# Moving small roundings, a subtraction and score copies from VectorE to ScalarE in a vision-transformer layer

## The reference

```python
h = relu(x @ W0.T) * (x @ W1.T) @ Wo.T          # token stage
h = concatenate([cls_tok, h])                   # 513 rows
h = h + attention(layernorm(h))                 # 16 heads of 16; every linear is quantised:
#   x_norm = (x - mean) * rsqrt(var + eps)      # mean, var over all rows of one image
#   y = round(x_norm * 127 / max|x_norm|) * max|x_norm| / 127  per row, times a ternary weight
h = h + moe(layernorm(h))                       # 8 experts, the best 2 of each row, silu(gate) * up
```

## Time and profile before

| | |
|---|---|
| median of 3 runs | 2325.64 us (2325.11 to 2326.09) |
| the profiled execution | 2323.41 us, span 2321.4 us |
| TensorE matmuls busy | 2018.8 us, 87% |
| TensorE weight loads busy | 1154.5 us, 50% |
| VectorE busy | 1572.5 us, 68% |
| ScalarE busy | 1235.4 us, 53% |
| GpSimd busy | 924.3 us, 40% |
| mean granted TensorE clock | 0.95 |

### The profile page before, as it was taken

The page is one execution under the profiler, slowest core; times in us unless marked ns, Lnnn a source line. Parts: engine busy times, 40 slices in busy tenths (PEclk is TensorE's granted clock), DMA queues, the critical chain, the costliest instruction groups (busy, mean ns, idle before and its releaser), DMA issues. The chain is left out here.

```text
span 2321.4 us, 49821 instructions
## 1 busy us (share of the span) xinstructions
PE 2018.8 (87%) x13328; PEld 1154.5 (50%) x13329; DVE 1572.5 (68%) x4268; ACT 1235.4 (53%) x2600; POOL 924.3 (40%) x958
## 2 busy tenths in 40 slices
PE   4789999898998998999989998884139999999997
PEld 2343443344443444444444443232128988888885
DVE  4477888887887888788787889973264444444443
ACT  0246666565665556656566566663145554545553
POOL 2222233433333234232342334333146666666653
PEclk9899999999999999999999999997569999999999
DMA  2312322223232223222232322310243333333331
GB/s 88 101 56 69 97 74 80 83 73 82 74 88 75 77 76 88 75 83 75 70 89 73 86 75 79 79 34 28 100 159 65 64 63 63 62 63 62 63 59 22
DMA packets 171886, 172.31 MB, mean 74 GB/s; under 512 B 30786, under 2 KB 160404, under 8 KB 171668
## 3 DMA queue, kind: packets, MB, share of 16 engines
q1 hardware_dynamic: 141396, 134.87, 20.1%
q0 software_dynamic: 30272, 34.80, 9.3%
HBM read 100.70 MB, written 68.99 MB: 73 GB/s over the span
## 5 line engine op out<-in xcount | busy, mean ns | idle before, releaser
L1162 DVE TENSOR_REDUCE mxs<-bank 128x1 f32<-128x512 f32 x1024 | 696.6, 684 | 218.1 <-PE bank L503 198.8
L833 ACT ACTIVATE pt<-bank 128x512 f32<-128x512 f32 x1024 | 588.5, 594 | 371.4 <-PE bank L512 368.2
L503 PE MATMUL bank<-ks,qs 96*128 96x512 bf16 x1024 | 400.2, 392 | 80.0 <-DVE mxs L1162 60.3
L512 PE MATMUL bank<-qs,ks 99*128 99x512 bf16 x1024 | 395.2, 387 | 9.8 <-ACT pt L833 9.2
L1780 PE MATMUL bank<-xh,gu_h 128*128 128x256 bf16 (+1 forms) x1152 | 309.6, 269 | 3.6 <-issue 1.9
L1780 PE MATMUL bank<-xl,gu_h 128*128 128x256 bf16 (+1 forms) x1152 | 308.4, 268 | 0.0
L1780 PE MATMUL bank<-xh,gu_l 128*128 128x256 bf16 (+1 forms) x1152 | 308.2, 268 | 0.0
L1740 POOL DMA_INDIRECT out<-y_sb,ids x136 | 217.2, 1597 | 203.2 <-ACT y_sb L1831 178.7
L521 PE MATMUL bank<-pt,v_sb 128*32 128x512 f32 x2048 | 279.5, 619 | 0.0
L503 PEld LDWEIGHTS bank<-ks,qs 96*128 96x128 bf16 x1024 | 103.7, 101 | 349.7 <-DVE mxs L1162 234.0
L1888 DVE TENSOR_TENSOR hid_e<-bank,act_g 128x256 f32<-128x256 f32 (+1 forms) x288 | 116.9, 406 | 170.0 <-PE bank L1780 166.5
(11 more groups left out here) (290 smaller groups left out, 3443.5 us busy)
## 6 DMA issues: line engine op xcount, KB each, us to landing
qs<-qk_dram SPq DMA_DIRECT2D x128, 128.0 KB, 2.6
ks<-qk_dram SPq DMA_DIRECT2D x64, 192.0 KB, 3.3
xt<-x_t SPq DMA_DIRECT2D x16, 512.0 KB, 3.9
h_dram<-h_sb SPq DMA_DIRECT2D x16, 512.0 KB, 3.5
qs<-qk_dram SPq DMA_DIRECT2D x128, 64.0 KB, 2.3
ks<-qk_dram SPq DMA_DIRECT2D x64, 128.0 KB, 3.3
hw<-h_dram SPq DMA_DIRECT2D x16, 512.0 KB, 4.2
out<-hw SPq DMA_DIRECT2D x16, 512.0 KB, 3.0
```

Of the source, the lines that this page charges most:

```text
L503: mm(score[u % 2][:, :], qs[0:QK, h, blk(t)], ks[0:QK, h, :], start=True, stop=True) \
L512: mm(scoret[u % 2][:, :], ks[0:QK + MROWS, h, blk(t)], qs[0:QK + MROWS, h, :], start=True, stop=True).then_inc(s("pe_st"), 1)
L833: f(pt[:, t % 2, j, :], scoret[u % 2][:, :], ACT.Exp).then_inc(s("act_exp"), 1)
L1162: v.reduce_max(mxs[:, t, g * GH + j:g * GH + j + 1], score[u % 2][:, :], AX.X).then_inc(s("dve_mx"), 1)
```

## The change

Four pieces of VectorE's work go to ScalarE; the numbers computed are the same.

- The negation of the maxima with its rounding (was L1172) is done by ScalarE at u = 0 of the next group, the second rounding (was L1179) at u = 2. VectorE forms `dsc` and `nmr` at u = 1 and the third part at u = 3.
- The three `scs` copies at slot 13 are done by ScalarE; `mc` stays on VectorE, at slot 14, after them.
- The subtraction of the mean from `oc` is done by ScalarE at slot 53, as an addition of `nms2` by its bias; the reduction moves to slot 54.
- The semaphores follow: VectorE's two chain semaphores of the maxima go, `dve_mf`, `act_nh`, `dve_nr`, `act_nm`, `act_scs`, `act_ocm` come.

```diff
@@ ScalarE
+                    if u == 0 and mt[0].ok:
+                        b, gg = mt
+                        wait(act, s("dve_mf"), NG, b, gg + 1)
+                        wait(act, s("pe_mt"), NG, b, gg)
+                        f(nmp[:, :, 0:GH], mf[:, :, heads(gg)], ACT.Copy, scale=-1.0).then_inc(s("act_nh"), 1)
+                    if u == 2 and mt[0].ok:
+                        b, gg = mt
+                        wait(act, s("dve_nr"), NG, b, gg + 1)
+                        f(nmp[:, :, GH:2 * GH], nmr[:, :, :], ACT.Copy).then_inc(s("act_nm"), 1)
...
+                    if C.ok and at == 13:
+                        wait(act, s("pe_t7"), 1, C, 1)
+                        wait(act, s("dve_dsc"), NG, C, -NG)
+                        for k in range(2):
+                            f(scs[:, C.par, k * TB * NH:(k + 1) * TB * NH].rearrange("p (a t h) -> p a t h", a=2, h=NH),
+                              d2[:, 0:S // 2].rearrange("p (t k a h) -> p k a t h", t=2, k=2, a=2)[:, k, :, :, 0:NH],
+                              ACT.Copy).then_inc(s("act_scs"), 1)
+                        f(scs[:, C.par, 2 * TB * NH:(2 * TB + 1) * NH], d2[:, S // 2:S // 2 + NH], ACT.Copy).then_inc(s("act_scs"), 1)
...
+                    if W.ok and at == 53:
+                        cflat = oc[:, :, :].rearrange("p j d -> p (j d)")
+                        wait(act, s("dve_nms2"), 1, W, 1)
+                        f(cflat, cflat, ACT.Identity, bias=nms2[0:NG, :]).then_inc(s("act_ocm"), 1)
@@ VectorE
-        def negate_maxima(b, g):
+        def largest(b, g):
             wait(dve, s("dve_mx"), UNITS * NG, b, UNITS * (g + 1))
-            ch = Link("dve_chain_m", NG * 4, b, 4 * g)
+            if g == 0:
+                wait(dve, s("act_scs"), 3, b, 3)
...
-            ch(v.tensor_tensor(mf[:, :, hs], mxs[:, :, hs], scl, ALU.max))
-            wait(dve, s("pe_mt"), NG, b, g)
-            ch.go(v.tensor_scalar(nmp[:, :, 0:GH], mf[:, :, hs], -1.0, None, ALU.mult))
+            v.tensor_tensor(mf[:, :, hs], mxs[:, :, hs], scl, ALU.max).then_inc(s("dve_mf"), 1)
         def maxima_rest(b, g):
-            ch = Link("dve_chain_m", NG * 4, b, 4 * g + 2)
-            ch.hold()
-            ch(v.scalar_tensor_tensor(nmr[:, :, :], mf[:, :, heads(g)], -1.0, nmp[:, :, 0:GH], ALU.mult, ALU.subtract))
-            ch.go(v.tensor_copy(nmp[:, :, GH:2 * GH], nmr[:, :, :]))
...
+            wait(dve, s("dve_mf"), NG, b, g + 1)
+            wait(dve, s("act_pcls"), NG, b, g + 1 - NG)
+            v.tensor_tensor(dsc[:, :, hs], scl, mf[:, :, hs], ALU.subtract).then_inc(s("dve_dsc"), 1)
+            wait(dve, s("act_nh"), NG, b, g + 1)
+            v.scalar_tensor_tensor(nmr[:, :, :], mf[:, :, hs], -1.0, nmp[:, :, 0:GH], ALU.mult, ALU.subtract) \
+                .then_inc(s("dve_nr"), 1)
         def maxima_low(b, g):
+            wait(dve, s("act_nm"), NG, b, g + 1)
             v.tensor_tensor(nmp[:, :, 2 * GH:3 * GH], nmr[:, :, :], nmp[:, :, GH:2 * GH], ALU.subtract).then_inc(s("dve_nm"), 1)
-            wait(dve, s("act_pcls"), NG, b, g + 1 - NG)
-            v.tensor_tensor(dsc[:, :, hs], scl, mf[:, :, hs], ALU.subtract).then_inc(s("dve_dsc"), 1)
...
-                    if u == 0 and mt[0].ok:
+                    if u == 1 and mt[0].ok:
                         maxima_rest(*mt)
-                    if u == 1 and mt[0].ok:
+                    if u == 3 and mt[0].ok:
                         maxima_low(*mt)
...
-                    if C.ok and at == 13:
-                        wait(dve, s("pe_t7"), 1, C, 1)
-                        for k in range(2):
-                            v.tensor_copy(scs[...], d2[...]).then_inc(s("dve_scs2"), 1)
+                    if C.ok and at == 14:
+                        wait(dve, s("act_scs"), 3, C, 3)
                         v.tensor_reduce(out=mc[:, :], in_=d2[:, CM_AT:CM_AT + 2 * VW].rearrange("p (a h) -> p h a", a=2)[:, 0:NH, :],
                                         axis=AX.X, op=ALU.max).then_inc(s("dve_mc"), 1)
-                        wait(dve, s("dve_scs2"), 2, C, 2)
-                        signal(v.tensor_copy(scs[:, C.par, 2 * TB * NH:(2 * TB + 1) * NH], d2[:, S // 2:S // 2 + NH]),
-                               "dve_scs", 1, C, 1)
...
-                    if W.ok and at == 53:
+                    if W.ok and at == 54:
                         cflat = oc[:, :, :].rearrange("p j d -> p (j d)")
-                        signal(v.tensor_scalar(cflat, cflat, ms2[0:NG, 0:1], None, ALU.subtract), "dve_ocm", 1, W, 1)
+                        wait(dve, s("act_ocm"), 1, W, 1)
                         wait(dve, s("pe_amc"), 1, W, 0)
```

More of the change, by code:

```diff
@@ L631, in body @@
                             if C.ok:
-                                wait(pe, s("dve_scs"), 1, C, 1)
+                                wait(pe, s("dve_mc"), 1, C, 1)
                             else:
@@ L1162, in head_max, with maxima_low @@
             v.reduce_max(mxs[:, t, g * GH + j:g * GH + j + 1], score[u % 2][:, :], AX.X).then_inc(s("dve_mx"), 1)
-        def negate_maxima(b, g):
+        def largest(b, g):
             wait(dve, s("dve_mx"), UNITS * NG, b, UNITS * (g + 1))
-            ch = Link("dve_chain_m", NG * 4, b, 4 * g)
+            if g == 0:
+                wait(dve, s("act_scs"), 3, b, 3)
             hs = heads(g)
             scl = scs[:, b.par, 0:TB * NH].rearrange("p (t h) -> p t h", t=TB)[:, :, hs]
-            ch(v.tensor_tensor(mf[:, :, hs], mxs[:, :, hs], scl, ALU.max))
-            wait(dve, s("pe_mt"), NG, b, g)
-            ch.go(v.tensor_scalar(nmp[:, :, 0:GH], mf[:, :, hs], -1.0, None, ALU.mult))
+            v.tensor_tensor(mf[:, :, hs], mxs[:, :, hs], scl, ALU.max).then_inc(s("dve_mf"), 1)
         def maxima_rest(b, g):
-            ch = Link("dve_chain_m", NG * 4, b, 4 * g + 2)
-            ch.hold()
-            ch(v.scalar_tensor_tensor(nmr[:, :, :], mf[:, :, heads(g)], -1.0, nmp[:, :, 0:GH], ALU.mult, ALU.subtract))
-            ch.go(v.tensor_copy(nmp[:, :, GH:2 * GH], nmr[:, :, :]))
-        def maxima_low(b, g):
             hs = heads(g)
-            ch = Link("dve_chain_m", NG * 4, b, 4 * g + 4)
-            ch.hold()
-            v.tensor_tensor(nmp[:, :, 2 * GH:3 * GH], nmr[:, :, :], nmp[:, :, GH:2 * GH], ALU.subtract).then_inc(s("dve_nm"), 1)
             scl = scs[:, b.par, 0:TB * NH].rearrange("p (t h) -> p t h", t=TB)[:, :, hs]
+            wait(dve, s("dve_mf"), NG, b, g + 1)
             wait(dve, s("act_pcls"), NG, b, g + 1 - NG)
             v.tensor_tensor(dsc[:, :, hs], scl, mf[:, :, hs], ALU.subtract).then_inc(s("dve_dsc"), 1)
+            wait(dve, s("act_nh"), NG, b, g + 1)
+            v.scalar_tensor_tensor(nmr[:, :, :], mf[:, :, hs], -1.0, nmp[:, :, 0:GH], ALU.mult, ALU.subtract) \
+                .then_inc(s("dve_nr"), 1)
+        def maxima_low(b, g):
+            wait(dve, s("act_nm"), NG, b, g + 1)
+            v.tensor_tensor(nmp[:, :, 2 * GH:3 * GH], nmr[:, :, :], nmp[:, :, GH:2 * GH], ALU.subtract).then_inc(s("dve_nm"), 1)
         def normalise(b, g):
@@ L1372, in body @@
                                                ALU.subtract, ALU.max).then_inc(s("dve_am"), 1)
-                    if C.ok and at == 13:
-                        wait(dve, s("pe_t7"), 1, C, 1)
-                        for k in range(2):
-                            v.tensor_copy(scs[:, C.par, k * TB * NH:(k + 1) * TB * NH].rearrange("p (a t h) -> p a t h", a=2, h=NH),
-                                          d2[:, 0:S // 2].rearrange("p (t k a h) -> p k a t h", t=2, k=2, a=2)[:, k, :, :, 0:NH]) \
-                                .then_inc(s("dve_scs2"), 1)
+                    if C.ok and at == 14:
+                        wait(dve, s("act_scs"), 3, C, 3)
                         v.tensor_reduce(out=mc[:, :], in_=d2[:, CM_AT:CM_AT + 2 * VW].rearrange("p (a h) -> p h a", a=2)[:, 0:NH, :],
                                         axis=AX.X, op=ALU.max).then_inc(s("dve_mc"), 1)
-                        wait(dve, s("dve_scs2"), 2, C, 2)
-                        signal(v.tensor_copy(scs[:, C.par, 2 * TB * NH:(2 * TB + 1) * NH], d2[:, S // 2:S // 2 + NH]),
-                               "dve_scs", 1, C, 1)
                     if P.ok and at in (16, 17):
@@ L1517, in body @@
                     if u == UNITS - 1 and C.ok:
-                        negate_maxima(C, g)
+                        largest(C, g)
         if stage == STEPS:
```

## The result

The changed kernel took 2306.44 us, the median of 6 runs (2300.94 to 2313.08), beside 2325.38 us for the kernel before on the same chip (6 runs, 2323.05 to 2330.11): a ratio of 0.9918 (0.9896 to 0.9940), 19 us. The forecast was 2315.4, a gain of 10.2 us; the time lies at the lower end of the stated range (2303 to 2325), where the third rival had put it (2304, chance 0.15).

What follows compares the result with a forecast made beforehand. TensorE was taken as the pace, with VectorE setting the end in a few places per image. Gains 3.6 + 4.7 + 1.5 + 2 = 11.8 us less 1.6 made 10.2, from 2325.64 to 2315.4 us; range 2303 to 2325.

Steps and rivals of the forecast that it cites:

- the two checks on ScalarE: Signs of error: VectorE waiting over 0.2 us for each ScalarE rounding, or vcls released by ScalarE's own queue instead of fk.
- L608's wait in image 3: Sign of the forecast: this weight load's wait for VectorE, 1.07 us before, would fall below 0.6.
- rival C: VectorE's stalls beside GpSimd vanish, and three images lose half-clock stretches with shorter TensorE waits: -21 us, 2304, chance 0.15.
- Slots 48 to 53: Second rounding gone ahead of TensorE's wait for slot 51's maximum: 0.28 us in 13 images, gain 3.6 us.
- Slots 63 to 3: Chain work cut where TensorE needs kbd and qbd: 0.59 us in half of 16 images, gain 4.7 us.
- Slots 53 to 58: VectorE level with TensorE sooner after the subtraction goes: 0.1 us per image, gain 1.5 us, bounds 0 and 22.
- item 3: Slot 53: the subtraction L1497, mean 1396 ns, leaves VectorE, removing 1.4 us of its time per image.
- Slot 13: Copies worth 0.4 us leave VectorE, but it waits for TensorE in slot 14, so gain 0.
- The charge for ScalarE: Twelve added ScalarE instructions per image, 0.22 us each, charged at 0.1 us per image, 1.6 us; bounds 0 and 42.
- Last two images: From 1400 to 1558 us, about a quarter of 8.4 us removed from VectorE lands: gain 2 us.
- A: TensorE reaches slot 53 earlier but then waits elsewhere, so a third of the sum arrives: -3.5 us, 2322, chance 0.20.
- B: Slots 0 to 6: ScalarE becomes late, the chain behind it slips 0.8 us per image: +7.3 us, 2333, chance 0.08.

Runs made afterwards that it cites:

- e1: Kernel before with only the two roundings of the maxima moved to ScalarE (L1178 and L1186 later): 2311.15 us against 2325.82, ratio 0.9936.
- e6: The whole change except the class query's subtraction, which stays on VectorE in slot 53: 2299.90 us against 2318.82 of the kernel before, ratio 0.9911.
- e7: The whole change except the class score copies, which stay on VectorE: 2300.58 us against 2318.82 of the kernel before, ratio 0.9916.
- e8: Changed kernel with each of the two roundings done a second time on ScalarE into an unread tile: 2300.54 us, ratio 0.9917 to the kernel before.
- e3: Kernel before with only the class score copies of slot 13 moved to ScalarE: 2314.92 us against 2325.82, ratio 0.9944.
- e9: Kernel before with one added VectorE memset of one column in slot 13: 2315.43 us against 2322.66, ratio 0.9968.
- e12: Kernel before with three added VectorE memsets of one column each in slot 13: 2320.40 us against 2328.93, ratio 0.9969.
- e2: Kernel before with only the class query's mean subtraction (slot 53) moved to ScalarE, its maximum to slot 54: 2315.50 us against 2325.82, ratio 0.9961.
- e4: Kernel before with both roundings kept on VectorE, the chain spread one instruction each over slots 0 to 3 of the group: 2315.96 us against 2325.82, ratio 0.9952.
- e5: Kernel before with its two class score copies of slot 13 in swapped order, no work removed: 2321.25 us against 2318.82, ratio 1.0011.
- e11: Changed kernel with row counter, output scale and router's weights moved to other VectorE slots: 2288.39 us, ratio 0.9851 to the kernel before.

## Why the prediction was half right

The direction and the bounding views were right, and so were the two checks on ScalarE: fk still releases vcls, and no wait for a rounding appears. L608's wait in image 3 came to 0.68 us, where below 0.6 was expected (1.07 before). The forecast itself was 9 us too slow, nearly half of the gain, and that the range held owes something to luck: it reached so far down because of rival C, and a part of the gain is granted clock and two pauses, which no term of the sum had. By its own steps:

**Slots 48 to 53** (-0.28 x 13 = -3.6). The size is exact inside the loop: -0.28 us in the even images of the changed kernel and of e1, e6, e7 and e8. Images 2 and 13, outside it, gave 0.09 us each, so 10 images in place of 13 had the full gain. What the step left out is the odd images, -0.64: 0.36 us more in five images (1.8 us), from a pause that e3 takes away too without touching this stretch, and behind it the half-clock stretches of images 3, 5 and 9, some 1.7 us each (5.0 us). e3 shows both without the roundings. The wait that I expected at 0.95 us was 0.58 for that reason.

**Slots 63 to 3** (half of the images at -0.59: -4.7). This is the term that failed most by size: slots 0 to 7 gave 9.0 us in the profiled execution, stretches at half clock included. That in image 10 VectorE again waits for TensorE at the maximum of slot 0, "and nothing is left", was the wrong end of the thought. In the even images of the kernel before stood a later wait that begins with VectorE's fk, over ScalarE's vcls and the exps behind it, in slot 6:

```profile
1033.12 0.39 PE L512 MATMUL bank<-qs,ks 99*128 99x512 bf16 x1 [0.69 <-ACT pt L833]
```

I had used the 4.1 us of these waits as the thing at risk from ScalarE, and not as something to gain. In the changed kernel they are 0.2 us in one place. Part of it comes back as a wait for GpSimd in slot 1, 1.13 us in every even image from 4 to 12, where it had been 0 in three of them and 1.0 in two. The net is -0.56 us in the even images. Of the odd ones image 3 shows -1.00 with no pause ahead of it, and image 13 -1.42, of which some 0.65 is the pause in slot 63 (e3, e9, e12).

**Slots 53 to 58** (item 3, -1.5, bounds 0 and -22). Right, at the lower bound: e2, corrected for the pause, shows 0.1 us per image in slots 56 to 63, and e6 without it is as fast as e7 with it. The 1.4 us stall is gone and did not move on to a neighbour; it was beside TensorE's work, and so hardly worth anything.

**Slot 13** (0). Right for the work: e3 changes nothing in even images. What e3 gained, 11 us, came by the moved pauses and by granted clock.

**The charge for ScalarE** (+1.6). It was most likely nothing. e8 put 27 us more of instructions on ScalarE at the same ratio; its interval of 4 us alone could hide 1.6, but its medians agree with the changed kernel's within 0.03 us in every group of eight slots up to slot 55. The added instructions stand in its wait for VectorE, and each holds up the next by 0.13, not 0.22 us.

**Last two images** (-2). Slots 48 to 55 of image 15 alone lost 3.8 us, and e1, e2 and e4 show 3.2 to 3.4 there; TensorE's waits for maxima in these images fell from 12.8 to 11.4 us. So the time moved with the clock stretches there more than with the waits.

**The rivals.** C's number was met, and one of its two reasons was right: three images did lose their stretch at half clock, and one of them is that of the earlier trace rows. Its other reason, the stalls beside GpSimd, was wrong for L1497: the stall went, at 0.1 us per image instead of the 0.4 of that rival. Where such stalls do cost TensorE 1.46 us, in slots 42 to 44, the change left them at three images of ten. The condition it named ("with shorter TensorE waits") is supported by four rows of image 9: waits of 1.22 and 1.22 us with a clock of 0.66 and 0.73 behind them, 0.87 with 1.00 (e3), and 0.58 in the changed kernel with

```profile
1000.22:1004.80 4.58, 4.58 (x26) 2.72 (x27) 3.99 (x14) 2.08 (x5) 4.03 (x5) 1.00 0.01 0
```

All profiled executions together bear it out for images 3 to 12: where the wait before slot 53 is 1.06 us or more (the odd images of the kernel before, e5, e9 and e12), a stretch at half clock follows in 8 of 20 cases; where it is 0.88 us or less, in none of 120. So in these executions no stretch came without the long wait, and the wait isn't sufficient: images 7 and 11 of the kernel before have it and no such stretch, nor has image 9 of e5. Nor did the change make the clock better as a whole: the mean granted clock is 0.951 like that of the kernel before, since stretches appeared in slots 45 and 46 of images 7 and 9 (some 3.3 of the +4.4 us in slots 40 to 47), both behind GpSimd's case, while e2 and e3 have 0.955 and 0.956. This is why the parts don't add up. Time multiplied by the mean clock, an estimate that counts a microsecond at half clock as half, is 2211 us for the kernel before beside e1 to e4, 2212 for e2 and e3, 2203 for e1; so e2 and e3 have only clock and e1 has 8 us of removed waiting. The memsets have nearly only clock, too: e9 gives 2207 beside 2209, e12 2213 beside 2211, where the last digit of the clock alone is worth 2 us. By the same product the changed kernel (2193) has some 14 to 18 us of it (the kernel before gives 2207 to 2211 on the three chips of e1 to e11). Of what it has more than e1, the pause in slot 38 of e1 is 1.8 us; the rest I can't say with these runs.

A (taken up elsewhere) was right only for the last part added. B (ScalarE late) fell: TensorE's waits for exps went from 4.1 to 0.2 us.

## What to carry to other kernels

Compare the same instruction in neighbouring rounds of a loop before pricing an edit: an idle time that alternates with the half of an unrolled body need not come from work or a dependence, and an edit that changes the number of instructions ahead can move it, so a gain or loss of this size needs a control that adds an instruction and nothing else. Then ask the control's trace where its gain lies; here most of it was not at the pause. Measure the effect of an edit per stage as a median over rounds without clock stretches, with the number of rounds that are left beside it, and the total only after that; totals of parts, here 36 us against 19, count the shared effects several times. And where TensorE waits for a second engine that waits for a third, work taken from the third can still count, even if its own next wait seems to end the matter.

## What the runs showed of the hardware that was not expected

- VectorE pauses 0.36 us longer than usual (0.49 in place of 0.13) at fixed places of its code, twice per two images in the kernel before. One instruction more ahead of it brought one pause to 0.33 us, three moved it five instructions up.
- With one small instruction more per image a kernel became 7 us faster (0.9968, 0.9957 to 0.9979), by granted clock (0.953 beside 0.951) and not by less work.
- A stretch at a granted clock of 0.5 behind TensorE's wait before slot 53 came in 8 of 20 images with a wait of 1.06 to 1.23 us, and in none of 120 with 0.18 to 0.88 us. Behind the long form of slots 42 to 44 one came in 10 of 45 images, behind the short form in none of 95.
- At the loop's back edge TensorE waits 2.3 to 5.3 us in slot 0 of images 5, 7, 9 and 11, in every kernel here. One row of the page of images 3 to 12 sums it, after the change:

```profile
PE bank L503 <- issue: 13.8, 4, 4.3
```

- ScalarE instructions of 128x16 elements take 0.21 us each and start 0.13 us apart (e8); VectorE's of the same shape take 0.17 us, and 1.12 us where one falls beside GpSimd's L1054. VectorE's 128x32 L1261 takes 0.19 us, and 1.09 beside L1043.
